# A blocked random-feature and phase kernel: the second pair of tiles turned by VectorE, GpSimd and DMA in place of TensorE

## The reference

```python
def attn(x):                       # x: 8192 tokens of 512
    ab, AB = xis, exp(xis)
    rfs = lambda v: AB / sqrt(512) * exp(v @ (ab[:, None] * proj).T - 0.5 * sum(v * v) * ab * ab)
    return rfs(x) @ rfs(input_weights).T
def ffn(x):
    real = x @ cos(theta + theta_noise)
    imag = x @ sin(phi + phi_noise)
    return sqrt(real * real + imag * imag)
x = layernorm(x + attn(x))
x = layernorm(x + ffn(x))
```

## Time and profile before

| | |
|---|---|
| median of 3 runs | 727.58 us (727.2 to 727.7) |
| the profiled execution | 728.28 us |
| its span, first to last instruction | 726.5 us |
| granted TensorE clock | 0.991 |
| busy: PE | 710.2 us (98%) |
| busy: DVE | 563.7 us (78%) |
| busy: ACT | 490.2 us (67%) |
| busy: POOL | 279.0 us (38%) |
| DMA packets | 32753, of which 3168 under 512 B; 60.80 MB |

### The profile page before, as it was taken

The page is one execution under the profiler, slowest core; times in us unless marked ns, Lnnn a source line. Parts: engine busy times, 40 slices in busy tenths (PEclk is TensorE's granted clock), DMA queues, the critical chain, the costliest instruction groups (busy, mean ns, idle before and its releaser), DMA issues.

```text
span 726.5 us, 10937 instructions
## 1 busy us (share of the span) xinstructions
PE 710.2 (98%) x3228; PEld 586.3 (81%) x3228; DVE 563.7 (78%) x963; ACT 490.2 (67%) x760; POOL 279.0 (38%) x465
## 2 busy tenths in 40 slices
PE   8998999999999999999999999999999999999993
PEld 7876888888888888888888888888888888888872
DVE  5699779787777868778786877869687777877686
ACT  6846757593957769395775939677594867757463
POOL 5765015606144260614416052341605235160525
PEclk9998999999999999999999999999999999999998
DMA  9761032320503222050322205032130503200011
GB/s 308 213 135 55 15 101 78 120 66 14 175 15 115 72 93 80 15 173 15 115 72 74 100 15 173 15 115 72 55 119 15 166 22 115 69 32 29 1 58 58
DMA packets 32753, 60.80 MB, mean 84 GB/s; under 512 B 3168, under 2 KB 3168, under 8 KB 32736
## 3 DMA queue, kind: packets, MB, share of 16 engines
q1 hardware_dynamic: 31584, 58.50, 24.4%
q0 software_dynamic: 1152, 2.10, 1.7%
HBM read 43.78 MB, written 16.81 MB: 83 GB/s over the span
## 4 chain that ended last, share of the span: by engine, by line
PE 92%; DVE 4%; POOL 1%; ACT 1%; issue 1%; POOLq 0%; ACTq 0%; DVEq 0%
PE token_ps L907 9%; PE token_ps L909 9%; PE token_ps L908 9%; PE token_ps L811 7%; PE token_ps L812 7%; PE token_ps L810 7%; PE project_ps L760 7%; PE project_ps L758 7%; PE project_ps L759 7%; PE turn_ps L821 4%; PE project_ps L907 3%; PE project_ps L909 3%; PE project_ps L908 3%; PE token_ps L838 1%; PE token_ps L839 1%; PE token_ps L840 1%
## 5 line engine op out<-in xcount | busy, mean ns | idle before, releaser
L398 POOL TENSOR_TENSOR late<-late 128x1024 f32<-128x1024 f32 x29 | 71.6, 2468 | 306.8 <-ACT late L668 306.8
L758 PE MATMUL project_ps<-xT_hi,gs_hi 128*128 128x512 f32 x248 | 100.1, 404 | 0.0
L810 PE MATMUL token_ps<-W_hi,F_hi 128*128 128x512 f32 x256 | 99.7, 389 | 0.0
L812 PE MATMUL token_ps<-W_hi,F_lo 128*128 128x512 f32 x256 | 99.6, 389 | 0.0
L811 PE MATMUL token_ps<-W_lo,F_hi 128*128 128x512 f32 x256 | 99.6, 389 | 0.0
L760 PE MATMUL project_ps<-xT_hi,gs_lo 128*128 128x512 f32 x248 | 97.2, 392 | 0.0
L759 PE MATMUL project_ps<-xT_lo,gs_hi 128*128 128x512 f32 x248 | 96.7, 390 | 0.0
L583 ACT ACTIVATE late<-late 128x1024 f32<-128x1024 f32 x29 | 30.8, 1062 | 77.1 <-POOL late L398 77.1
L668 ACT ACTIVATE late<-late 128x1024 f32<-128x1024 f32 x54 | 57.2, 1059 | 33.0 <-DVE late L1397 28.8
L643 ACT ACTIVATE z<-z,shift,rstd 128x512 f32<-128x512 f32 x56 | 45.2, 807 | 40.0 <-POOL shift L393 40.0
L1135 DVE TENSOR_TENSOR z<-token_ps,x_tok 128x512 f32<-128x512 f32 x64 | 44.2, 690 | 31.4 <-PE token_ps L812 28.1
(11 more groups left out here) (214 smaller groups left out, 1809.5 us busy)
## 6 DMA issues: line engine op xcount, KB each, us to landing
x_tok<-in_x SPq DMA_DIRECT2D x16, 1024.0 KB, 5.5
out_tokens<-o_tile SPq DMA_DIRECT2D x62, 256.0 KB, 2.2
plain_xT_lo<-in_xT SPq DMA_DIRECT2D x14, 1024.0 KB, 5.3
norm_bc<-token_norms SPq DMA_DIRECT2D x15, 256.0 KB, 3.2
plain_T_hi<-in_gsT SPq DMA_DIRECT2D x4, 256.0 KB, 4.1
z<-in_wT SPq DMA_DIRECT2D x4, 256.0 KB, 4.4
plain_T_lo<-in_xT SPq DMA_DIRECT2D x1, 1024.0 KB, 7.7
plain_T_hi<-in_theta SPq DMA_DIRECT2D x4, 256.0 KB, 6.5
```

What stands on the lines that cost most here:

```text
L398: pool.tensor_tensor(parts[:, p, :, 0, :], parts[:, p, :, 0, :], parts[:, p, :, 1, :], ALU.add).then_inc(sum_made, 2)
L758: nc.tensor.matmul(o, gs_hi[:, c, cols], rhs_hi[:, c, :], start=(c == 0), stop=False)
L810: nc.tensor.matmul(o, F_hi[:, c, cols], W_hi[:, c, :], start=(c == 0), stop=False)
L812: return nc.tensor.matmul(o, F_lo[:, c, cols], W_hi[:, c, :], start=False, stop=(c == C - 1))
```

## The change

In blocks 2 to 14 (the steps with `more`) tiles 2 and 3 aren't transposed by TensorE. VectorE turns both, 32 x 32 squares in place each, with one instruction (`turn_squares`) from z into the part `late[:, 4:6]`. The squares must then change their places: square (i, k) of the 4 x 4 grid goes from partitions 32 i on to partitions 32 k on. The four with i = k are copied by GpSimd (`keep_squares`). The twelve others are DMA transfers of 32 partitions x 8 x 32 elements, so 256 runs of 128 bytes each, eight issued by SyncE and four by ScalarE (`move_squares`). They write into zT_raw, the plain view of zT_lo, in a new order of the blocks (MOVED_HALVES). ScalarE rounds from there (`round_moved_first`, `round_moved_sums`), and VectorE takes half sums and lower halves from there (`moved_half_sums`, `split_moved_first`, `split_moved_sums`) and no longer from PSUM. The first pair and the last block are turned as before.

The negated mean of the first norm goes from GpSimd to VectorE (`negate_mean1`), and the statistics of tiles 1 and 3 come before VectorE's other work. ScalarE norms tile 3 right behind tile 2 and loads the exponentials' table after `round_first(0)`. GpSimd's loop over blocks is written out.

```diff
@@ SyncE
+            def move_squares(b):
+                sp.wait_ge(squares_turned, b - PLAIN + 1)
+                for i, k in MOVES[:MOVES_BY_SP]:
+                    src, dst = square_move(i, k)
+                    sp.dma_start(dst, src).then_inc(halves_moved[0], 16)
@@ step
                     store_out(b - 1, 2)
                     store_out(b - 1, 3)
+                if moved:
+                    move_squares(b)
                 if ahead:
                     sp.wait_ge(project_done, C * (b + 3))
@@ shared
+        def square_move(i, k):
+            src = turned_squares[32 * i:32 * i + 32].rearrange("r t (c k s) -> r (t c) k s", c=C, s=32)
+            dst = zT_raw[32 * k:32 * k + 32, 1, 0:4 * Q].rearrange("r (c i s) -> r c i s", c=2 * C, s=32)
+            return src[:, :, k, :], dst[:, :, i, :]
+        MOVES = [(i, k) for i in range(P // 32) for k in range(P // 32) if i != k]
+        MOVES_BY_SP = 8
@@ GpSimd
             def scale1(b, j):
                 root1(b, j)
-                pool.tensor_tensor(neg_mean[:, j:j + 1], mv[:, j, 0:1], minus_one[:, 0:1], ALU.mult).then_inc(neg_mean_made, 1)
+            def keep_squares(b):
+                pool.wait_ge(squares_turned, b - PLAIN + 1)
+                for i in range(P // 32):
+                    src, dst = square_move(i, i)
+                    pool.tensor_copy(dst, src).then_inc(halves_kept, 1)
                 scale1(b, 3)
+                if more:
+                    keep_squares(b)
                 pair_sum(b, 0)
@@ ScalarE
+                def move_squares():
+                    act.wait_ge(squares_turned, s + 1)
+                    for i, k in MOVES[MOVES_BY_SP:]:
+                        src, dst = square_move(i, k)
+                        act.dma_start(dst, src).then_inc(halves_moved[1], 16)
+                def round_moved_first():
+                    for moved, credit in zip(halves_moved, MOVE_CREDITS):
+                        act.wait_ge(moved, credit * (s + 1))
+                    act.wait_ge(halves_kept, (P // 32) * (s + 1))
+                    nc.scalar.activation(zT_hi[:, 1, 0:2 * Q], zT_raw[:, 1, 0:2 * Q], ACT.Copy).then_inc(halves_hi_made, 1)
@@ step
                 if more:
-                    load_table(ACT.Exp)
                     norm1(1)
                     norm2(b - 1, 2)
                     norm2(b - 1, 3)
                     norm1(2)
+                    norm1(3)
                     round_first(0)
+                    load_table(ACT.Exp)
                     features(C * (b + 2), 0, 0)
+                    move_squares()
                     round_second(0)
-                    norm1(3)
                     features(C * (b + 2) + 1, 1, 1)
                     round_half_sums(0)
                     features(C * (b + 2) + 2, 2, 0)
-                    round_first(1)
-                    round_second(1)
                     features(C * (b + 2) + 3, 3, 1)
+                    round_moved_first()
                     copy_first(0)
-                    round_half_sums(1)
                     load_table(ACT.Sqrt)
...
+                    round_moved_sums()
@@ TensorE
                         if j < 2:
                             turn(b, j)
-                    turn(b, 2)
-                    turn(b, 3)
@@ VectorE
+                def turn_squares():
+                    dve.wait_ge(out_made, C * (b - 1) + 3)
+                    dve.wait_ge(z_made, C * b + 4)
+                    nc.vector.transpose(turned_squares, z[:, 2:4, :]).then_inc(squares_turned, 1)
@@ step
                 stats1(b, 1)
                 stats1_made(b, 1)
+                negate_mean1(b, 0)
+                moments1(1)
+                negate_mean1(b, 1)
                 pair_residual2(b - 1, 1)
-                moments1(1)
...
                     moments1(2)
                     stats1(b, 3)
+                    stats1_made(b, 3)
+                    negate_mean1(b, 2)
+                    moments1(3)
+                    negate_mean1(b, 3)
                     dve.wait_ge(norms_loaded, 16 * (b + 2 - NORMS_ON_PE + 1))
-                    stats1_made(b, 3)
                     next_exponent(b, slot, 0)
-                    moments1(3)
+                    turn_squares()
                     split_first(0)
...
                     next_exponent(b, slot, 3)
-                    split_first(1)
-                    split_second(1)
-                    half_sums(1)
+                    moved_half_sums()
+                    split_moved_first()
                     join_u(0)
                     join_v(0)
                     join_c22(0)
                     join_w(0)
-                    split_half_sums(1)
                     join_c11(0)
+                    split_moved_sums()
```

More of the change, by code:

```diff
@@ L284, in _, with step @@
             fetch_norms(2, 0)
-            def step(b, slot, ahead, first=False):
+            def step(b, slot, ahead, first=False, moved=False):
                 if not first:
@@ L313, in _ @@
                 for slot in range(2):
-                    step(pair * 2 + slot, slot, True)
+                    step(pair * 2 + slot, slot, True, moved=True)
             for slot in range(2):
-                step(NB - 2 + slot, slot, False)
+                step(NB - 2 + slot, slot, False, moved=(slot == 0))
             store_out(NB - 1, 0)
@@ L440, in step @@
                 scale1(b, 3)
+                if more:
+                    keep_squares(b)
                 pair_sum(b, 0)
                 pair_residual2(b, 0)
-            with pool.Fori(PLAIN, NB) as b:
-                step(b)
+            for b in range(PLAIN, NB):
+                step(b, b < NB - 1)
             pool.wait_ge(square_done, 2 * C * NB + SQUARE_CREDIT - 1)
@@ L698, in step @@
                         act.wait_ge(x_loaded[slot], 16 * (pair + 2))
-                        for j in range(C):
-                            sum_square(b + 3, j, slot, 1 - slot)
+                        sum_square(b + 3, 0, slot, 1 - slot)
+                        sum_square(b + 3, 1, slot, 1 - slot)
+                    round_moved_sums()
+                    if ahead:
+                        sum_square(b + 3, 2, slot, 1 - slot)
+                        sum_square(b + 3, 3, slot, 1 - slot)
                         act.wait_ge(xT_loaded, 16 * (b + 3))
@@ L895, in second_step, with half @@
                     last.then_inc(phase_done, 1)
-            def half(p, k):
+            def half(p, name, moved):
+                k = (MOVED_HALVES if moved else HALVES).index(name)
                 cols = [slice(k * Q + i * P, k * Q + (i + 1) * P) for i in range(H)]
@@ L927, in pair_products @@
                             pe.wait_ge(joined, joins_done(b, 0, join_order, "C11"))
-                        quarter_product(token_ps[0][:, :], half(p, 0), quarter(cos_hi, cos_lo, 0))
+                        quarter_product(token_ps[0][:, :], half(p, "A11", moved), quarter(cos_hi, cos_lo, 0))
                     if name == "M6":
@@ L954, in pair_products @@
                     if name == "M4":
-                        pe.wait_ge(halves_lo_made, 4 * s + 2 * p + 2)
+                        if not moved:
+                            pe.wait_ge(halves_lo_made, 3 * s + 2 * p + 2)
                         if p == 1:
@@ L965, in pair_products @@
                             pe.wait_ge(expo_made, C * (b + 2) + 4)
-                        quarter_product(project_ps[1][:, :], half_sum(p, "S4"), quarter(low_sin_hi, low_sin_lo, 0))
+                        quarter_product(project_ps[1][:, :], half(p, "S4", moved), quarter(low_sin_hi, low_sin_lo, 0))
             def step(b, more, behind_plain=False):
@@ L1356, in half_sums @@
                     tt(S4, A12, S2, ALU.subtract).then_inc(half_sums_made, 1)
+                def half_sums(p):
+                    sum_halves(p, turn_ps[0][:, 0:Q], turn_ps[0][:, Q:2 * Q], zT_raw[:, p, 6 * Q:7 * Q], turn_ps[1][:, Q:2 * Q],
+                               *[zT_raw[:, p, (3 + k) * Q:(4 + k) * Q] for k in range(4)])
                 def split_half_sums(p):
```

59 lines of the change are left out of this document (41 added, 18 removed).

## The result

| kernel | us (median, lowest to highest) | ratio to before, 95% interval |
|---|---|---|
| before | 727.64 (727.2 to 728.6) | |
| changed | 737.22 (736.54 to 737.59) | 1.0124 [1.0112, 1.0137] |

The change makes the kernel slower by 9.6 us. The prediction was 725.4 us and faster. The profiled execution took 736.86 us, its span is 734.7.

A forecast was written before the change was run, and what follows sets the result against it. TensorE, with 92% of the chain, was taken as the bound. Per step 0.87 us gained less 0.7 of waits (0.3 + 0.1 + 0.3) left 0.17, 2.2 us in 13 steps: 727.58 to 725.4 us; range 718 to 738.

The forecast's parts named there:

- TensorE's side of the sum: Dropping eight transposes of tiles 2 and 3 saves TensorE 0.87 us a step, 11.3 us in 13 steps.
- the price of the four transfers: ScalarE's issues before rounding the first pair's second tile: 1.6 us, of which its arithmetic feels 0.1.
- The cover: ScalarE's table load and exponentials, under which its four transfers are issued, from 315.4 to 317.0.
- The bound of 1.8 us: Upper limit of what ScalarE's arithmetic feels of its four transfers, if nothing covers them; lower limit 0.
- M6's 0.3 us of wait: TensorE's second product of the first pair (M6) waits 0.3 us for half sums' lower halves, ending at 322.0.
- first rival: ScalarE's arithmetic stands still while its four transfers are issued: in full 745 us, half of it 735; chance 0.24.
- the main case: Whole run, centred at -2.2 us (725.4 us), spread 721.5 to 729.3; chance 0.52.
- The rest of ScalarE's chain: ScalarE's norms, store wait, rounding, table load and exponentials put rounding of the first pair's second tile at 317.1, not 315.46.
- GpSimd's 1.2 us: GpSimd instruction held up by VectorE's two-operand SBUF addition; the same 1.2 us is paid one or two instructions further on.
- The smaller waits: TensorE waits 0.1 us at the fifth product (ScalarE's copy) and 0.2 to 0.3 at the second pair's second product.
- The hidden things: SyncE's eight transfers (315.4 to 318.7), packets, landing near 320.8 and GpSimd's copies cost TensorE nothing; 4 us of cover.
- third rival: Moved squares land too late for VectorE's second-pair half sums: at 60 ns a packet, 784 us; chance 0.08 with other new-path faults.

The follow-up runs named there:

- all_by_sync: Changed kernel with all twelve transfers issued by SyncE and none by ScalarE: 725.15 us, ratio 0.9966 to the kernel before.
- last_negation_sooner: All transfers on SyncE, table load early; in the last block the first tile's negated mean precedes the second tile's residual addition: 721.83 us, ratio 0.9927 to before.

## Why the prediction was wrong

**The gain was there.** From tile 1's addition to M1 a step took 321.18 - 303.29 = 17.89 us and takes 321.82 - 304.74 = 17.08: 0.81 of the 0.87 us. TensorE's side of the sum was right.

**The step that failed is the price of the four transfers.** I took 1.6 us for the four, from the row of a load out of DRAM and four stores of norms, and concluded that under the table load and the exponentials "the arithmetic feels 0.1 us". Measured: 2.60 us for the four, and 0.88 felt. The start (316.62, beside the table load) was right within 0.2 us, and so was the end of the exponentials: 318.48 stands for 317.03 on the old step's clock (1.45 less, by the addition at 304.74 for 303.29), where 317.0 was forecast. The cover, forecast from 315.4 to 317.0, was as long as the forecast issues, which left no room for a wrong price; it came out at 1.86 us, and 2.60 less that, with 0.12 from the last issue to the rounding, is the 0.88. The bound of 1.8 us came from rows of another kind of transfer as well. With the right price `round_second` starts 0.78 us later than the sum had it, and M6's 0.3 us of wait become 1.1; 1.14 was measured. The sign named for the first rival, M6 waiting over 1 us with a gap of ScalarE at the transfers, came as written. all_by_sync, which hands just these issues to SyncE, gave 725.15.

**The first rival** (ScalarE feels its transfers, 0.24, half of it 735) is what came, 737.2. That the number lies within the range of 718 to 738 is owed to the half of this rival that the range took in; the main case, 721.5 to 729.3, missed it. Its reasons don't hold. The sequencer didn't come late: ScalarE's first issue starts 0.03 us behind the turn. As for sharing: the page of the Trainium skill that the prediction cites (Perfetto Trace Analysis, DMA Instruction — HWDGE) says that the generator is locked for exclusive use until all descriptors of an issue are made. It doesn't say how much of an issue that is. If it were nearly all of it, ScalarE's issues would be quicker alone and two queues no quicker together. Here ScalarE's take 632 ns in the median with SyncE beside it and 632 without, and together the two queues issue twelve in 5.6 us, SyncE alone in 7.9. So the measurement excludes a lock over the whole issue; a short one, that makes the other queue wait now and then, fits SyncE's second issue (0.85 for 0.60 us) and the loads from DRAM (0.56 and 0.63 us for 0.47), and no run here tests it. In either case it is not what ScalarE lost its 0.88 us to.

**The rest of ScalarE's chain** came as written: the norm of tile 2 waits for the store (0.86 us, start at 310.84 on the old clock for 311.1), table load at 314.3 for 314.4, the turn 1.25 us for 1.25. GpSimd's 1.2 us was met one instruction further on (L431, 1.28 us at 306.64), also as written.

**The smaller waits** were 0.1 and 0.2 to 0.3 in the sum (its own terms add up to 326.18 and not 326.25, so the first is nearer 0). Between M1 and the second M1 lie 10.86 us for 9.61, so 1.25: M6's 1.14 and 0.11 more. Behind it come 0.1: the mean step is 0.58 us longer, and 1.25 - 0.81 = 0.44 of that is accounted for.

**The hidden things** stayed hidden, one by less than thought. SyncE's eight took 5.6 us and not 3.3, the last landed at 323.5, and they were wanted at 326. The third rival (squares land late) did not come about; two kernels that push the landing later (842 and 762 us) show how steep it is there, the slower clock behind TensorE's waits included. GpSimd's copies took 1.75 us.

**A step that was left out.** The sum has thirteen steps and nothing for block 15. The negated mean's move costs 1.6 us there, and last_negation_sooner gave 1.2 of them back.

Together: 725.4 + 13 x 0.78 = 735.5, and 1.6 for the last block gives 737.1; measured 737.2. So near a match is luck. By the spans the changed kernel ended 10.4 us behind the forecast (8.2 more in place of 2.2 less), where these two terms make 11.7: the start of the program, with block 2's step, got shorter and not longer. The medians lie 9.6 us apart and the spans 8.2, which makes up the difference. That all_by_sync comes out at the forecast 725 confirms less than it seems to. It still carries the 1.6 us of the last block, and its step is 42.30 us where 42.68 - 0.17 = 42.5 was forecast: M6 starts 0.13 us late there and not 0.3.

## What to carry to other kernels

Price a transfer's issue by a row of the same kind, source and destination alike; if there is none, let the range reach to where the cover ends, and count how many issues fit between their signal and the next thing the issuing engine must do: here ScalarE's first two were free and the third and fourth cost 12 us. Take transfers off the engine that feeds the bound before doubting anything else, and when the later landing starts to be felt, give back as many as fit. Walk an edit through every step that runs it, the last one too, where the work that hid it is missing.

## What was not expected of the hardware

- Issuing a transfer within SBUF costs 0.59 to 0.63 us in the median, whatever its bytes (16 or 32 KB), its runs (32, 128 or 256) and its queue; out of DRAM into the same place, with no other queue issuing, the first of four costs 0.32 and the others 0.47.
- SyncE and ScalarE issue such transfers at the same time almost without slowing each other: 626 for 611 ns in the median on SyncE, 632 for 632 on ScalarE. Only SyncE's second of a step is dearer, 0.85 for 0.60 us.
- Squares issued beside or just behind the load of a megabyte on the other queue land after 5.0 to 5.9 us, the one issued just ahead of it after 1.9.
- Behind a wait of 6.8 us TensorE ran some 4 us at the slower of its two levels, its matmuls 0.43 us apart for 0.23.
